# Self attention of the second block: four score products in one group, output and residual a batch later

## The reference

```python
q = split_heads(x @ Wq + bq); k = split_heads(x @ Wk + bk); v = split_heads(x @ Wv + bv)
q = _rope(q); k = _rope(k)
scores = jnp.einsum('bhqd,bhkd->bhqk', q, k) / np.sqrt(D_K)
probs = jax.nn.softmax(scores, axis=-1)
attn = jnp.einsum('bhqk,bhkd->bhqd', probs, v)
out = attn.transpose(0, 2, 1, 3).reshape(B, S, D_MODEL) @ Wo + bo
x = _layernorm(x + out)
```

## Time and profile before

| | value |
|---|---|
| median of three runs | 2146.33 us |
| lowest and highest | 2144.48 and 2150.35 us |
| the profiled execution's own time | 2144.02 us |
| its span | 2142.3 us |
| mean granted TensorE clock | 0.948 |
| PE, PEld busy | 1938.4 us (90%), 1503.1 us (70%) |
| DVE, ACT, POOL busy | 1433.7 (67%), 1188.2 (55%), 502.1 us (23%) |

### The profile page before, as it was taken

The page is one execution under the profiler, slowest core; times in us unless marked ns, Lnnn a source line. Parts: engine busy times, 40 slices in busy tenths (PEclk is TensorE's granted clock), DMA queues, the critical chain, the costliest instruction groups (busy, mean ns, idle before and its releaser), DMA issues.

```text
span 2142.3 us, 47704 instructions
## 1 busy us (share of the span) xinstructions
PE 1938.4 (90%) x16935; PEld 1503.1 (70%) x16935; DVE 1433.7 (67%) x3525; ACT 1188.2 (55%) x3926; POOL 502.1 (23%) x812
## 2 busy tenths in 40 slices
PE   3548999999999999999869999979999688699998
PEld 1227888888888888888647777757776455467776
DVE  4776777777777777777456757568887599444443
ACT  2215666666666777666425445447777466133333
POOL 2101111111111111111122212034444377111110
PEclk8668999999999999999889999989999899599999
DMA  8000000000000000000200000010000000000000
GB/s 217 24 0 2 2 2 2 2 2 2 2 2 2 2 2 2 2 2 2 70 1 1 1 1 1 1 36 2 2 2 2 26 17 2 1 0 11 6 5 20
DMA packets 29438, 25.64 MB, mean 12 GB/s; under 512 B 5260, under 2 KB 25748, under 8 KB 29208
## 3 DMA queue, kind: packets, MB, share of 16 engines
q1 hardware_dynamic: 29208, 22.62, 3.9%
HBM read 20.52 MB, written 2.10 MB: 11 GB/s over the span
## 4 chain that ended last, share of the span: by engine, by line
issue 60%; PE 21%; POOL 11%; POOLq 6%; DVE 1%; DMA 1%; ACT 0%; DVEq 0%; SPq 0%; ACTq 0%
PE bank L1414 3%; PE bank L1423 3%; POOL X L1822 3%; PE bank L1435 3%; POOL work L946 2%; PE bank L1943 2%; PE bank L1930 2%; PE bank L1932 2%; POOLq L949 1%; PE bank L1406 1%; POOL H L950 1%; POOL work L934 1%; POOL work L1039 1%; PE bank L1910 1%; POOLq L1821 1%
## 5 line engine op out<-in xcount | busy, mean ns | idle before, releaser
L814 ACT ACTIVATE work<-bank,work 128x128 f32<-128x128 f32 x1024 | 364.6, 405 | 223.8 <-DVE work L867 223.8
L694 PE MATMUL bank<-work,wbig 128*128 128x128 f32 x2048 | 261.8, 276 | 0.6 <-ACT work L855 0.5
L814 ACT ACTIVATION_READ_ACCUMULATOR work<-bank,work 128x1 f32 x1024 | 250.4, 245 | 0.0
L694 PEld LDWEIGHTS bank<-work,wbig 128*128 128x128 f32 x2048 | 245.5, 193 | 1.2 <-ACT work L855 0.8
L874 DVE TENSOR_TENSOR work<-work 128x512 f32<-128x512 f32 x256 | 177.3, 692 | 24.4 <-issue 6.4
L867 DVE TENSOR_REDUCE work<-bank 128x4 f32<-128x512 f32 x256 | 158.9, 683 | 33.7 <-PE bank L733 33.7
L829 ACT ACTIVATE work<-bank 128x512 f32<-128x512 f32 x256 | 170.4, 666 | 13.2 <-PE bank L707 13.2
L707 PE MATMUL bank<-ident,work 128*128 128x128 f32 x1024 | 156.4, 276 | 3.0 <-DVE work L874 3.0
L1481 ACT ACTIVATE work<-bank,work 128x128 f32<-128x128 f32 x512 | 147.6, 389 | 9.2 <-DVE work L1513 9.2
L2103 DVE TENSOR_TENSOR work<-wff,bank 128x320 f32<-128x320 f32 (+1 forms) x128 | 62.5, 489 | 128.0 <-ACT wff L2018 127.5
L707 PEld LDWEIGHTS bank<-ident,work 128*128 128x128 f32 x1024 | 119.2, 141 | 40.3 <-issue 19.0
(11 more groups left out here) (283 smaller groups left out, 4053.7 us busy)
## 6 DMA issues: line engine op xcount, KB each, us to landing
wbig<-in_moe_w SPq DMA_DIRECT2D x2, 1536.0 KB, 9.3
work<-in_mask_l SPq DMA_DIRECT2D x8, 256.0 KB, 2.8
out<-X SPq DMA_DIRECT2D x8, 256.0 KB, 2.3
H<-in_moe_w SPq DMA_DIRECT2D x3, 512.0 KB, 5.5
wff<-in_moe_w SPq DMA_DIRECT2D x1, 1024.0 KB
wbig<-in_sa_wq SPq DMA_DIRECT2D x1, 512.0 KB, 3.6
wbig<-in_sa_wk SPq DMA_DIRECT2D x1, 512.0 KB, 4.4
wbig<-in_sa_wv SPq DMA_DIRECT2D x1, 512.0 KB, 5.5
```

The source lines that it names most:

```text
L694: last = nc.tensor.matmul(o[:, j * T:(j + 1) * T], w[:, t * 128:(t + 1) * 128], src, start=True, stop=True)
L814: last = nc.scalar.activation(at_probs[:, g, h, :], bank[g][:, h * T:(h + 1) * T], ACT.Exp, bias=at_nmax[:, g, h:h + 1], accum_out=at_den[ ...
```

## The change

`score` no longer has pairs: all four products are issued at the head of step t, behind one wait, with one signal. In the step, TensorE's order becomes scores of t, transposes 3 of t-1, output of batch t-2 with the v product of t, projections of t+2, tokens, transposes 0 of t, weighing of t-1, transposes 1 and 2 of t. ScalarE copies transposes 3 of t-1 first, then does exponentials 0 and 1, the tokens copy, copy 0, exponentials 2 and 3, copy 1. VectorE does the residual's sum of batch t-2 between maxima 1 and 2 and its statistics behind maxima 3; the loops of TensorE, VectorE and GpSimd run one step longer. `weigh` waits for the values of the batch behind (`v_sb`) and for the residual of the one ahead (`res_sum`).

```diff
-            def score(b, pair):
+            def score(b):
                 pe.wait_ge(l1.kblk, b + 1)
-                need(pe, l1.probs, QUAD * (b - 1) + 2 * pair + 2)
-                for i in (2 * pair, 2 * pair + 1):
+                need(pe, l1.probs, QUAD * b)
+                for i in range(QUAD):
...
                 pe.wait_ge(l1.xT_sb, min(b + 4, B - 1) + 1)
-                pe.wait_ge(l1.v_sb, b + 1)
+                pe.wait_ge(l1.v_sb, min(b + 2, B))
+                need(pe, l1.res_sum, b)
...
-            for t in range(-3, B + 1):
+            for t in range(-3, B + 2):
                 now = 0 <= t < B
                 if now:
-                    score(t, 1)
-                if t >= 1:
+                    score(t)
+                if 1 <= t <= B:
                     turn(t - 1, 3)
+                output(t - 1)
+                if 0 <= t + 2 < B:
+                    project(t + 2)
                 if t + 3 < B:
                     tokens(t)
-                if 0 <= t + 2 < B:
-                    project(t + 2)
                 if now:
                     turn(t, 0)
-                if t >= 1:
+                if 1 <= t <= B:
                     weigh(t - 1)
                 if now:
                     turn(t, 1)
-                if 0 <= t + 1 < B:
-                    score(t + 1, 0)
-                output(t)
-                if now:
                     turn(t, 2)
...
             for t in range(-3, B + 1):
                 now = 0 <= t < B
-                if now:
-                    exps(t, 0)
                 if t >= 1:
                     turned(t - 1, 3)
+                if now:
+                    exps(t, 0)
+                    exps(t, 1)
                 if t + 3 < B:
                     tokens(t)
                 if now:
-                    exps(t, 1)
                     turned(t, 0)
                     exps(t, 2)
+                    exps(t, 3)
                     turned(t, 1)
-                    exps(t, 3)
...
             def greatest(b, g):
-                dve.wait_ge(l1.scores, 2 * b + g // 2 + 1)
+                dve.wait_ge(l1.scores, b + 1)
...
                 nc.vector.tensor_tensor(l1_res[b % 2], bank[7][:, 0:D], l1_xb[b % 2], ALU.add).then_inc(l1.res_sum, 1)
+
+            def stats_(b):
                 dve.drain()
...
-            for t in range(-2, B + 1):
+            for t in range(-2, B + 2):
                 now = 0 <= t < B
-                if t >= 1:
-                    turned(t - 1)
+                if now:
+                    greatest(t, 0)
+                    greatest(t, 1)
+                    values(t)
+                if t >= 2:
+                    residual(t - 2)
                 if now:
                     greatest(t, 2)
                     greatest(t, 3)
+                if t >= 2:
+                    stats_(t - 2)
                 if 0 <= t + 2 < B:
                     rope(t + 2)
-                if t >= 1:
+                if 1 <= t <= B:
                     heads(t - 1)
-                if 0 <= t + 1 < B:
-                    greatest(t + 1, 0)
-                    greatest(t + 1, 1)
-                if t >= 1:
-                    residual(t - 1)
-                if 0 <= t + 1 < B:
-                    values(t + 1)
+                if now:
+                    turned(t)
...
-                need(pool, l1.scores, 2 * (b - 1))
+                need(pool, l1.scores, b - 1)
...
-            for t in range(-2, B + 1):
+            for t in range(-2, B + 2):
+                if t >= 2:
+                    inv(t - 2)
                 if 0 <= t + 2 < B:
                     keys(t + 2)
-                if 0 <= t + 1 < B:
-                    biased(t + 1)
-                if t >= 1:
-                    inv(t - 1)
+                if 0 <= t < B:
+                    biased(t)
```

More of the change, by code:

```diff
@@ L1496, in attn1_act @@
                 now = 0 <= t < B
+                if t >= 1:
+                    turned(t - 1, 3)
                 if now:
                     exps(t, 0)
-                if t >= 1:
-                    turned(t - 1, 3)
+                    exps(t, 1)
                 if t + 3 < B:
```

## The result

The changed kernel takes 2143.05 us (median of 20 runs, 2140.17 to 2147.04), the kernel before, in as many runs beside it, 2148.19 us (2140.77 to 2151.15). The medians differ by 5.1 us; the ratio is 0.9979 with a 95% interval of 0.9972 to 0.9987: about 4.5 us less, 3 to 6. The forecast was 4.2 us less. The profiled execution took 2141.83 us with a span of 2140.1.

A forecast was written before the change was run, and what follows sets the result against it. TensorE's own order, 7.69 us a batch, was taken to bound the kernel; 1.4 (steady part) + 1.9 (end) + 0.9 (start) = 4.2 us off the 2146.33 us median gave 2142.1 us, range 2134 to 2149.

The forecast's parts named there:

- Four products in one group: TensorE's score group: four products take 1.07 us, as in the next stage, so 1.06 us a batch leaves TensorE.
- rival C: The four score products don't run side by side and cost 2.12 us; time 2170 us, chance 0.02.
- The loop closes at the weighing's wait for the tokens copy: Steady part: scores, transposes 3, their copy, exponentials 0 and 1, tokens copy, then weighing; copy ends at 4.53 us.
- Rival A: TensorE's order alone bounds again, period 6.44 to 6.5 us; 36.6 us less, 2109.7 us, chance 0.12.
- The size of the period: One batch in the steady part takes 7.64 us, ends 7.53 and 7.74, against 7.69 before.
- The restart of 0.20: Delay from the end of ScalarE's tokens copy to TensorE's weighing: 0.20 us, with 0.09 and 0.30 as ends.
- the steady part: 27 batches at 7.64 instead of 7.69 us: 1.4 us less, from 4.3 less to 1.4 more.
- Start and end: Stage's start up to the first weighing gains 0.9 us (0 to 1.2); its last weighings gain about 1.9 us.
- a period of 6.96: Last four weighings, where no tokens are left: the tokens copy leaves the loop and a batch takes 6.96 us.
- VectorE's edges: VectorE's maxima start 1.18 us behind the scores; the forecast is wrong if later than 1.3.
- Rival B, the clock: TensorE's waits could bring stretches at granted clock 0.50; with 40 us of them 2158 us, chance 0.08.
- The total: Whole kernel: 4.2 us less, ends about 0.5 and 7.4, all from the changed stage; 2142.1 us.

The follow-up runs named there:

- tokens_early: Changed kernel, but ScalarE copies the tokens between exponentials 0 and 1 instead of behind exponentials 1; 2134.96 us, ratio 0.9932 to the kernel before.
- extra_after: Changed kernel with two of the four projection products issued twice, 0.44 us more TensorE work a batch; 2145.49 us, ratio 0.9984 to the kernel before.

## Why the prediction was right, and where it was not

- **Four products in one group cost 1.07.** Right, and rival C with its 2.12 is out. The 3.07 of the page "TensorE: Matmul & The Clock Gate" of the Trainium skill (section "Part 3: Packing small matmuls") led to an estimate of 1.16; this case measured 1.07.
- **The loop closes at the weighing's wait for the tokens copy.** Right: `tokens_early` removes it by one place in ScalarE's order, and `extra_after` shows the slack of TensorE that the loop leaves. Rival A, the full gain of 36 us, fails as the forecast said it would.
- **The size of the period.** 7.64 forecast, 7.71 measured, within the ends of 7.53 and 7.74 that were given. The mis-sized term is the tokens copy: I took 0.27 from the single copy in the earlier trace rows, it takes 0.34 behind eight exponentials. The restart of 0.20 was exact. 0.07 over 27 batches is the 1.9 us by which the steady part missed: 1.4 less was forecast, 0.5 more came.
- **Start and end.** -1.06 for -0.9 and -1.63 for -1.9. The start is close in part by luck: I followed it at the clock of before, and TensorE was 3.4 us less at half clock. How much would be left at the clock of before, no run shows. After the last tokens I expected a period of 6.96; the steps are 6.97, then twice 7.13, then 4.91.
- **VectorE's edges.** Right: maxima start 1485.88 - 1484.67 = 1.21 behind the scores (forecast 1.18, wrong if above 1.3).

```profile
1485.88 1.29 DVE L1511 TENSOR_REDUCE work<-bank 128x4 f32<-128x512 f32 x2 [0.18 <-PE bank L1414]
```

- **Rival B, the clock.** It didn't come: 1.00 with TensorE busy for 53.10 of 60 us.
- **The total.** 4.2 forecast and 4.5 measured agree by luck: 2.2 are in the stage, and the rest goes with the clock in the stage behind, of which the forecast said that it would only start earlier or later. With the stage alone the total would have been about half of the forecast.

## What to carry to other kernels

When work is taken off the engine that bounds a written-out pipeline, walk one item round the loop of waits with the durations of the trace: the sum of TensorE's steps (6.44 here) is only a floor, and the loop (7.71) is what this kernel got. The cheapest experiment is then to move one instruction past its neighbour on the engine that the loop names: here one copy ahead of four exponentials took 10.6 us off the stage, while the saved matmuls had taken 2.2. Compare the changed stage by itself, too: of the 4.0 us between the profiles here, 1.8 lay in stages whose code had not changed. And put only those waits in front of a late instruction that nothing ahead of it has covered.

## What was not expected of the hardware

Activations in an unbroken run are recorded longer: the tokens copy took 0.271 on average (28 of them) in the kernel before, 0.28 behind a copy and four exponentials in `tokens_early`, and 0.338 (8 of them) behind eight exponentials in the changed kernel, and a group of four exponentials starts every 1.00 us but takes 1.14 alone and, as a half of the later eight, 2.26 - 1.00 = 1.26:

```profile
L1491 ACT ACTIVATE work<-bank 128x128 f32<-128x128 f32 x8 | 2.7, 338 | 0.0
```

```profile
L1493 ACT ACTIVATE work<-bank 128x128 f32<-128x128 f32 x28 | 7.6, 271 | 0.0
```

The starts are not delayed, only the ends, so it costs where somebody waits for the last one, as the weighing does here. The other figure worth having was already in the earlier trace rows and holds here too: four products of 32 partitions take 1.07 together, two take 1.06.
